# Two-layer block in float32: the steps from the down projection to the self product cut by feature chunk and placed ahead of the heads' copies

## What is computed

```
x = x + gate_msa * (attn_out @ proj_w + proj_b)
h = _rms(x) * (1.0 + scale_mlp) + shift_mlp
mlp = silu(h @ w1_w) * (h @ w3_w) @ w2_w
x = x + gate_mlp * mlp
...
row_zero = exp_v.sum(-1) == 0
q_exp = where(row_zero[..., None], 0.0, q[:, None, :])
vcq = concatenate([exp_v, q_exp], axis=-1)
self_feat = vcq @ W_self.T + b_self
...
qh = self_feat @ Wq.T + bq;  kh = self_feat[:, :20] @ Wk.T + bk
...
return exp_v + relu(output)
```

## Time and profile before

| | |
|---|---|
| median of 3 runs | 1422.27 us (1420.46 to 1423.88) |
| profiled execution, span from first to last instruction | 1416.1 us |
| busy share of the span | PE 95%, DVE 80%, ACT 62%, POOL 50% |
| one trip of the loop | 41.4 us (the scores start at 322.19 and, 14 trips later, at 901.84) |
| granted TensorE clock, mean | 0.977 of full |

### The profile page before, as it was taken

The page is one execution under the profiler, slowest core; times in us unless marked ns, Lnnn a source line. Parts: engine busy times, 40 slices in busy tenths (PEclk is TensorE's granted clock), DMA queues, the critical chain, the costliest instruction groups (busy, mean ns, idle before and its releaser), DMA issues.

```text
span 1416.1 us, 51305 instructions
## 1 busy us (share of the span) xinstructions
PE 1342.2 (95%) x20276; PEld 1229.1 (87%) x20276; DVE 1135.2 (80%) x2033; ACT 878.6 (62%) x1752; POOL 712.1 (50%) x612
## 2 busy tenths in 40 slices
PE   4679999999999999999999999999999999999985
PEld 3578899999998999999898999999999999999974
DVE  5667888888888888888888888888888888888753
ACT  4556666666666666666666666666666666656542
POOL 0235555455655544555555455555545555554541
PEclk8589999999999999999999999999999999999998
DMA  7001111010111101111110111111011111100100
GB/s 240 29 23 30 45 43 43 18 38 30 43 43 43 43 15 36 34 43 43 43 43 15 35 35 43 43 43 43 15 33 37 43 43 43 43 15 28 30 22 16
DMA packets 49827, 56.19 MB, mean 40 GB/s; under 512 B 4352, under 2 KB 47744, under 8 KB 49792
## 3 DMA queue, kind: packets, MB, share of 16 engines
q1 hardware_dynamic: 48944, 53.86, 12.1%
q10 hardware_dynamic: 848, 1.84, 0.4%
HBM read 47.03 MB, written 8.65 MB: 39 GB/s over the span
## 4 chain that ended last, share of the span: by engine, by line
PE 73%; issue 9%; POOL 7%; ACT 3%; DVE 1%; ACTq 0%; POOLq 0%; DVEq 0%
PE psum L486 39%; PE psum L607 5%; PE psum L622 5%; PE psum L728 4%; PE psum L792 4%; PE psum L758 4%; PE psum L775 3%; POOL nl L1315 3%; PE psum L587 3%; PE psum L806 2%; POOL gl L1315 2%; POOL kbd L1327 2%; ACT gh L926 1%; PE psum L534 1%; ACT qkT L892 1%
## 5 line engine op out<-in xcount | busy, mean ns | idle before, releaser
L1315 POOL TENSOR_TENSOR gl<-gf,gh 128x512 fp32r<-128x512 f32 x96 | 124.3, 1295 | 260.4 <-ACT gh L926 260.4
L486 PE MATMUL psum<-nh,w_lo 128*128 128x256 f32 x704 | 182.2, 289 | 0.0
L486 PE MATMUL psum<-nh,w_hi 128*128 128x256 f32 x704 | 176.8, 282 | 0.0
L1315 POOL TENSOR_TENSOR nl<-xn,nh 128x512 fp32r<-128x512 f32 x64 | 99.2, 1551 | 127.3 <-ACT nh L864 127.3
L486 PEld LDWEIGHTS psum<-nh,w_lo 128*128 128x128 f32 x704 | 132.8, 189 | 1.0 <-issue 1.0
L486 PEld LDWEIGHTS psum<-nh,w_hi 128*128 128x128 f32 x704 | 133.0, 189 | 0.0
L1379 POOL TENSOR_TENSOR e<-e,inv 128x640 f32<-128x640 f32 x64 | 82.0, 1282 | 87.6 <-DVE inv L1271 87.6
L486 PE MATMUL psum<-nl,w_hi 128*128 128x256 f32 x704 | 115.4, 282 | 0.0
L926 ACT ACTIVATE gh<-gf 128x512 fp32r<-128x512 f32 x96 | 60.3, 628 | 61.6 <-DVE gf L1201 60.8
L486 PEld LDWEIGHTS psum<-nl,w_hi 128*128 128x128 f32 x704 | 97.5, 188 | 0.0
L486 PE MATMUL psum<-qkv_lo,nh 128*128 128x512 f32 (+1 forms) x256 | 88.5, 356 | 2.8 <-ACT nh L864 2.8
(11 more groups left out here) (186 smaller groups left out, 4382.4 us busy)
## 6 DMA issues: line engine op xcount, KB each, us to landing
adj<-in_adj SPq DMA_DIRECT2D x32, 440.0 KB, 3.3
x_in<-in_x SPq DMA_DIRECT2D x32, 256.0 KB, 2.7
xn<-in_xT SPq DMA_DIRECT2D x32, 256.0 KB, 3.6
x_res<-in_xT SPq DMA_DIRECT2D x32, 256.0 KB, 3.7
out_T<-y SPq DMA_DIRECT2D x32, 256.0 KB, 2.2
e<-in_adaln ACTq DMA_DIRECT2D x2, 512.0 KB, 5.4
stage<-in_qkv SPq DMA_DIRECT2D x2, 384.0 KB, 5.0
pT<-in_w SPq DMA_DIRECT2D x2, 384.0 KB, 6.4
```

What stands on the lines that cost most here:

```text
L486: last = nc.tensor.matmul(out, lhsT, rhs, start=start and i == 0, stop=stop and i == len(terms) - 1)
L1315: return nc.gpsimd.tensor_tensor(out, full, hi.bitcast(F32), ALU.subtract)
```

## The change

The four steps between the down projection and the self product (gate, add, high part, low part) are made for each feature chunk by itself: four instructions of 128 x 512 become eight of 128 x 256, and the four signals count to `DC`. All other users of these signals wait for both chunks. On PE the row sums of the low part, with the wait for it, move ahead of the high products of the second output chunk. `score` waits for a tile's copies ahead of that tile rather than for both tiles' at the start. In the lists, ACT makes `x2_split` ahead of both heads' copies, and POOL makes it ahead of both spreads of the keys.

```diff
@@ ORDER @@
     "Activation": [
-        (2, "rope_scale", 0), (0, "mlp_split", 2), (1, "mixT", 0), (2, "heads", 0), (2, "heads", 1),
-        (0, "x2_split", 0), (0, "self", 0), (1, "norm1_mean", 0), (0, "keys", 0), (0, "self_split", 0),
+        (2, "rope_scale", 0), (0, "mlp_split", 2), (1, "mixT", 0), (0, "x2_split", 0),
+        (2, "heads", 0), (2, "heads", 1), (0, "self", 0), (1, "norm1_mean", 0), (0, "keys", 0), (0, "self_split", 0),
...
@@ signals @@
-        down_done, down_gated = signal("down_done"), signal("down_gated")
-        x2_done, x2_hi, x2_lo = signal("x2_done"), signal("x2_hi"), signal("x2_lo")
+        down_done, down_gated = signal("down_done"), signal("down_gated", DC)
+        x2_done, x2_hi, x2_lo = signal("x2_done", DC), signal("x2_hi", DC), signal("x2_lo", DC)
@@ PE, score @@
-                wait(pe, qkT_kept, m, TILES)
-                wait(pe, k_spread, m, TILES)
...
                 for t in range(TILES):
+                    wait(pe, qkT_kept, m, t + 1)
+                    wait(pe, k_spread, m, t + 1)
                     for c in range(DC):
@@ PE, self_feat @@
-                wait(pe, x2_hi, m, 1)
+                wait(pe, x2_hi, m, DC)
...
-                for o in both:
-                    linear(self_out[:, o, :], high_terms("self", out_chunks[o], nh[1], both), o == 0, False)
-                wait(pe, x2_lo, m, 1)
+                linear(self_out[:, 0, :], high_terms("self", out_chunks[0], nh[1], both), True, False)
+                wait(pe, x2_lo, m, DC)
                 linear(rowsum_ps, [(ones_r[:, 0:M_SUM], nl[1][:, c, :]) for c in both], start=False).then_inc(rowsum.sem, 1)
+                linear(self_out[:, 1, :], high_terms("self", out_chunks[1], nh[1], both), False, False)
@@ ACT, x2_split @@
-                wait(act, x2_done, m, 1)
-                nc.scalar.activation(nh[1][:, :, :], x2[:, :, :], ACT.Copy).then_inc(x2_hi.sem, 1)
+                for o in range(DC):
+                    wait(act, x2_done, m, o + 1)
+                    nc.scalar.activation(nh[1][:, o, :], x2[:, o, :], ACT.Copy).then_inc(x2_hi.sem, 1)
@@ DVE, mlp_down @@
-                nc.vector.tensor_tensor(by_seq(x2[:, :, :]), by_seq(down_ps),
-                                        per_seq(mods[:, GATE_M:GATE_M + DC, bass.ds(m * MB, MB)]), ALU.mult).then_inc(down_gated.sem, 1)
+                for o in range(DC):
+                    nc.vector.tensor_tensor(by_seq(x2[:, o:o + 1, :]), by_seq(down_ps[:, o:o + 1, :]),
+                                            per_seq(mods[:, GATE_M + o:GATE_M + o + 1, bass.ds(m * MB, MB)]), ALU.mult)\
+                        .then_inc(down_gated.sem, 1)
@@ POOL, mlp_down and x2_split @@
-                wait(pool, down_gated, m, 1)
-                nc.gpsimd.tensor_tensor(x2[:, :, :], x2[:, :, :], x1[:, :, :], ALU.add).then_inc(x2_done.sem, 1)
+                for o in range(DC):
+                    wait(pool, down_gated, m, o + 1)
+                    nc.gpsimd.tensor_tensor(x2[:, o, :], x2[:, o, :], x1[:, o, :], ALU.add).then_inc(x2_done.sem, 1)
...
-                wait(pool, x2_hi, m, 1)
-                low_part(nl[1][:, :, :], x2[:, :, :], nh[1][:, :, :]).then_inc(x2_lo.sem, 1)
+                for o in range(DC):
+                    wait(pool, x2_hi, m, o + 1)
+                    low_part(nl[1][:, o, :], x2[:, o, :], nh[1][:, o, :]).then_inc(x2_lo.sem, 1)
```

More of the change, by code:

```diff
@@ L109 @@
         (3, "norm0_scale", 0), (1, "norm1_apply", 0), (3, "norm0_apply", 0), (0, "soft1", 0), (1, "mlp_up", 0),
-        (0, "soft1", 1), (1, "edges", 0), (1, "mlp_up", 1), (1, "mlp_up", 2), (1, "mlp_down", 0), (3, "heads", 0),
-        (1, "x2_split", 0), (3, "heads", 1),
+        (0, "soft1", 1), (1, "edges", 0), (1, "mlp_up", 1), (1, "mlp_up", 2), (1, "mlp_down", 0), (1, "x2_split", 0),
+        (3, "heads", 0), (3, "heads", 1),
     ],
@@ L575, in score @@
             def score(m, n):
-                wait(pe, qkT_kept, m, TILES)
-                wait(pe, k_spread, m, TILES)
                 wait_free(pe, m, (g_done, -2, 3), (pT_b, -1, 2))
-                wait_free(pe, m, (down_gated, -2, 1), (v_kept, 0, 2))
+                wait_free(pe, m, (down_gated, -2, DC), (v_kept, 0, 2))
                 wait_free(pe, m, (proj_gated, -1, 2), (cos_part, 0, 1))
@@ L766, in score1 @@
                 wait_free(pe, m, (shifted_s, 2, 2), (g_done, 0, 3))
-                wait_free(pe, m, (shifted_s, 2, 2), (down_gated, 0, 1))
+                wait_free(pe, m, (shifted_s, 2, 2), (down_gated, 0, DC))
                 wait_free(pe, m, (shifted_s, 2, 2), (proj_gated, 1, 2), (biased1, -1, 4))
@@ L956, in self_split @@
                 wait(act, self_done, m, DC)
-                wait(act, x2_lo, m, 1)
+                wait(act, x2_lo, m, DC)
                 nc.scalar.activation(nh[1][:, :, :], sf[:, :, :], ACT.Copy).then_inc(self_hi.sem, 1)
```

## The result

| | before | after |
|---|---|---|
| median of the runs | 1423.08 us (1420.46 to 1425.49, 4 runs) | 1402.88 us (1400.84 to 1407.77, 4 runs) |
| profiled execution, span | 1416.1 us | 1398.9 us |
| one trip of the loop, median of 27 | 41.40 us | 40.96 us |
| granted TensorE clock, mean | 0.977 | 0.977 |

The ratio is 0.9868, with a 95% interval of 0.9847 to 0.9889: 1.3% faster. The forecast was 1409.2, the range 1401 to 1421. A trip is measured from the start of one block's first row sum product on PE (`nh,ones_r`) to that of the next; the 27 trips are those of the loop without the ones at its ends.

The account below looks back on a forecast made before the run. PE, busy 95%, was taken as the bound, with DVE's chain also on the path; 30 blocks of 0.40 (12.0) plus 1.1 at the end gave 13.1, so 1422.27 becomes 1409.2 us, range 1401 to 1421.

Parts of the forecast that it names:

- the 0.43 forecast: Ahead of the first q product's low part, PE would newly wait 0.43 us for Pool, leaving PE a gain of 0.36.
- Pool's chain: Residual add of x1, ACT's squares, self split, Pool's low part: claimed to end last, letting PE load at 739.71 against 740.07.
- the eight matmuls: Two low row sums on PE ahead of cond, claimed to hide the row gate, so PE reaches cond at 734.81.
- A Pool half: One 256-column Pool instruction of the rewritten stretch: claimed 0.74 us, with a step of 0.70 to the next.
- rival (a): Shorter Pool halves, 0.62 a step: a block gains 0.72, total 1399.6 us; chance 0.13 for 1399 to 1405.
- rival (d): Slower: hand-offs make each Pool step longer, no gain at 0.80, about 1433 us at 0.90; chance 0.09.
- Rival (b): Pool yields to DVE at the squares' add, losing 0.25: 1415.2 us; chance 0.15, shared with other small gains, 1413 to 1419.
- Rival (c): No change: some chain behind the stretch is as tight as PE's, 1422 or 1421 us; chance 0.13.
- DVE's account: DVE's chain from the scores, with two steps waiting under Pool: claimed gain 0.40 us a block, 12.0 for 30 blocks.
- the maximum at 737.15: DVE's scores' maximum, claimed to start at 737.15 against 737.55, after edge steps that wait under Pool's x1 add until 736.7.
- The wait per tile: At the scores: claimed to buy nothing itself, its two extra waits possibly costing 0.1 on a piece with slack.
- The last blocks: Last two blocks, without a heads step: halves and earlier low row sums claimed to gain 1.1 us for both.

Follow-up runs that it names:

- cutting the chain at ACT: Changed kernel with ACT's keys copy and self split moved ahead of its squares of x1: 1395.25 us, ratio 0.9809, trip 40.64.
- the second execution: Changed kernel measured and profiled once more with nothing edited: 1403.22 us, ratio 0.9862, trip 40.96.
- the wait's runs: Changed kernel with both scores' waits up front again: 1415.82 us; kernel before with only the scores' wait per tile added: 1420.6 us.

## Why the prediction was right, and where it was not

**What bounds the kernel, and where the gain is lost.** Right in the main. The hole at the low row sums is gone, the new wait is on Pool's `nl` at `q` (0.33 of idle time for the 0.43 forecast), and the gain on PE behind it is 0.36, as said. Pool's chain ends last: one more Pool instruction costs 0.14 a trip, and cutting the chain at ACT gives 0.32. One reading on the way was off: cond was to follow hidden behind the eight matmuls, at 734.81, and came at 735.01 (720.90 + 14.11), although the row gate started at 734.16, as forecast. So the scores gained 0.74 and not 0.9. It cost nothing, since PE had to wait at `q` all the same, and the run with the row sums moved back shows it: there the hole at cond is back and the trip is 40.96.

**A Pool half.** Right: 0.74, and a step of 0.70. That settled rival (a), which needed 0.62, and rival (d), which needed more than 0.80. Rival (b) is out too, since Pool's self low part kept 1.29. Rival (c) had some chain behind as tight as PE's; the trip fell to 40.96.

**DVE's account.** The mechanism holds and its size was too small: 0.42 to 0.45 in place of 0.40. The step that failed is the maximum at 737.15. I let `edge_bias` run after the residual's add had ended, but it ends with it, and the maximum came at 736.82 (722.71 + 14.11), 1.38 behind the first load of the scores, where it stands 1.34 behind it with the edge steps moved away: PE set it, and the edge steps at most 0.04 of it. The squares' add then started sooner and waited longer (0.73), and the next maximum stood at 739.86 against 740.28. Over the 27 trips the 0.05 is 1.4 us.

**The wait per tile.** Wrong, and the main miss of the sum: its part at the head was put at nothing. I wrote that it buys nothing because the second copy ends at 735.58 and the second tile is reached at 735.85. That compares the copy with the wrong moment: a wait up front holds the start of the scores, 735.3, until 735.58, and the waits behind it then take their half microsecond with nothing to cover them. Taken back, it costs 0.31 a trip. And I looked for it in the loop alone. At the head PE had waited 2.37 for both copies, and 2.9 us went there, in part through the clock.

**The last blocks.** The 1.1 us for both did not show: the two last steps took 36.60 and 36.16 us, where they took 36.47 and 35.37, and the profile of the second execution has 36.79 and 35.11. The stretch behind them took 34.0 in place of 31.5, with a granted clock of 0.57 and 0.83 in its first ten microseconds. The other kernels fall on either side of this too: 31.3 to 31.6 us with the row sums moved back, with the longer Pool chain and in both of the wait's runs, 33.0 to 34.4 in the rest that ran at this pace. What sorts them is the clock in those ten microseconds: 0.83 in every kernel with 31.3 to 31.6, 0.55 to 0.58 in those with 34.0 to 34.4, 0.68 in the one with 33.0. No part of the change sorts the clock, so I leave the cause of the tail open.

**The sum.** 27 trips of 0.45 are 12.2 of the 17.2 us between the spans; the head gives 3.1, the first two trips 5.3 (of which 4 were there or not in two profiles of the same kernel), and the end takes 3.4 back. The spans fell by 4.1 more than the 13.1 of the forecast: 3.1 is the head, 1.4 the term of DVE, and the first trips and the end, for which the forecast had 2.3 together, gave 1.9. The median is 6.3 below the forecast, since 2.2 more lie in what I added to the span: 6.2 before, and 4.0 after. That the sum came this near is in part luck: the first trips give 4 us that another execution of the same kernel doesn't, and the end takes 3.4 back. And 1402.88 lies where I had put rival (a), whose shorter Pool half wasn't there.

## What to carry to other kernels

A wait that covers two things is to be priced at the moment when the wait stands, not at the moment when the second thing is used, and at the program's head too, where nothing hides it. Splitting steps and moving them can each lose alone and gain together, so the order in which the lists are then followed without a hole is what is to be costed. Of a moved step count the buffers that it frees and the queue that waits for them, and look which engine comes first at each meeting with Pool. Look at the single trips and at their clock, not only at their median.

## What the runs showed of the hardware

- DVE's elementwise instructions that read only SBUF and started under a running Pool instruction ended 0.06 to 0.55 behind it, one with a single tensor input too (`edge_n`, 0.18 to 0.20 clear of Pool and 1.11 under it). `edge_bias` went from 0.30 to 1.20 to 1.24, the squares' add from 0.42 to 0.73, the norm's shift from 0.69 to 1.55. The reduction of 880 columns took 1.05 in either place, and the norm's product with a PSUM input kept its 0.68 under Pool.
- It holds the other way round: Pool's low part of the norm took 1.69 in place of 1.28 when it started 0.15 behind DVE's shift.
- Two-input instructions of Pool took 195 ns with 2 columns, 737 to 740 with 256 and 1286 with 512.
- The granted clock was low around and behind long waits of PE: 0.51 over the 7 us that hold the end of an idle time of 6.3, and 0.59 over the 4 us behind one of 1.54, the latter in 12 of 27 trips with the same wait.
- Two executions of one kernel, with like times in all, differed by 4.3 us in the first trip of the loop.
